# The first four attention pairs of a layer take their rows straight from the projected parts in SBUF

## The chip, the cores and the metric

The kernel runs on one core of a Trainium2 chip. The metric is the device time of one execution in microseconds (us): the median of three runs before the change is 1721.19 us (1714.81 to 1726.53).

## What is computed

The input x is 2 batches of 1024 tokens with 128 features. The reference applies an ffn layer to it, then a top-k attention layer, then the same ffn layer again. The part of the ffn layer that the change touches is its causal attention with 16 heads of 8 features:

```
q, k, v = split(x @ w_qkv)                     # 16 heads x 8 features each
scores  = q . k / sqrt(8), causal mask         # 1024 x 1024 for each of 2 x 16 heads
attn    = softmax(scores);  o = (attn . v) @ w_o
h       = layernorm(x + o);  then 8 experts (w1, gelu, w2), weighted by the top 2 of the gate
```

The kernel runs the ffn layer twice (c = 0 and c = 1), the top-k attention lies between the two.

## The kernel before, in words

**Pairs.** Two heads of one batch are a pair, and a layer has 16 pairs. A pair's queries and keys stand as "rows" of two SBUF tiles, QB and KB, [128 x 1024] each (ring of RING = 4, tiles ffn_65 to 68 and ffn_69 to 72 in the trace's names). A number is split in two fp32r parts (high and low), and the product of all parts is made by 32 contraction rows for each head: for one head QB holds each of 2 x 8 part rows twice, KB holds its 16 part rows in two copies. Behind them are 3 rows in which the row maxima are subtracted.

**How the rows come to be.** L880 and L882 multiply x by w_qkv; ScalarE (L1242) writes the high parts and VectorE (L1561, counter low_done) the low parts to qparts and kparts (ffn_49 and ffn_50), in which feature h*8+d of head h is a partition. After four of its eight blocks the first batch is complete (two of them are the queries, two the keys). `sp_spill` writes the parts of one batch to memory (q_rows, k_rows: 2 MB for a batch), and `sp_rows` loads a pair's rows from there, with the repetition that the layout wants: for each head 128 KB into QB (L475), 128 KB into KB (L476) and three zero rows (L477). A last transfer (L482) copies the pair's 72 KB of values into VS. `sp_rows` of the first pair waits until the whole spill of batch 0 has landed.

**The work on a pair.** Pass 1 (`pe_pass1`, L769 and L776; 9 units) makes scores whose maxima VectorE takes (L1468, L1478). VectorE then reduces them to row maxima (L1486), GpSimd splits these into three bf16 parts (L687 to L694), TensorE turns them (L785), ScalarE copies them (L1216, counter mt_ready), and SyncE's queue stores them to QB's three rows (`sp_maxrows`, L489, two transfers of 12 KB). Only then pass 2 may run: `pe_scores` (L802), exp on ScalarE (L1207), the causal cut on GpSimd (L708) and `pe_values` (L824).

**What sets the order at a layer's start.** TensorE runs the 9 pass 1 units of pair 0 and 4 of pair 1, then turns pair 0's maxima and waits for their rows. From there the pieces of pair n's pass 2 and pair n+1's and n+2's pass 1 alternate in a fixed order. All transfers of this part are issued by SyncE, in program order, to one hardware queue (q1) that is served by 16 DMA engines; a transfer that is issued later stands behind the earlier ones on the engines that it uses. In layer 0 SyncE also issues before all this the experts' first weights, the top-k attention's weights, and bb1: the experts' biases, 4096 elements of 4 bytes each (L564). In layer 1 it issues the first experts' weights (1 MB) ahead of the spill.

**GpSimd's part.** `pool_fill` clears QB and KB of all four ring places and writes ones into KB's three rows, one place after the other (counter filled).

## Time and profile before

| | |
|---|---|
| median of three runs | 1721.19 us |
| profiled execution, its own time | 1717.98 us |
| its span | 1715.8 us |
| TensorE busy | 1417.6 us, 83% of the span |
| VectorE / ScalarE / GpSimd busy | 1242.0 / 998.4 / 447.7 us |
| chain that ended last | PE 60%, DVE 11%, ACT 9%, DMA 6%, issue 6%, SPq 3% |

The span is the profiled execution's time from its first to its last instruction. TensorE is the engine that sets most of the end, but what this change touches are two stretches in which it stands still: in layer 0 between 20 and 85 us, in layer 1 between 1186 and 1249 us. Times in rows are us from the span's start. "PEclk" is the granted share of TensorE's clock (1.00 is 2.4 GHz, 0.50 is 1.2 GHz).

### The profile page before, as it was taken

What the parts mean: (1) busy time and instruction counts of PE and PEld (TensorE: products, weight loads), DVE (VectorE), ACT (ScalarE), POOL (GpSimd) and SP (SyncE); (2) the same over time, 40 slices, a digit from 0 to 9 for tenths busy, and PEclk for the clock granted to TensorE, in tenths of its full rate; (3) what the DMA queues carried; (4) which work ended last, traced back from release to release, by engine and by line L of the source; (5) the groups of instructions that cost most, each with busy time, mean ns of one, the idle gap of its engine ahead of it and who ended that gap; (6) DMA issues with size and microseconds to landing.
All of it is one profiled execution on the core that took longest, in us unless ns stands there. A gap on an engine that the chain in (4) does not pass through costs nothing.

```text
span 1715.8 us, 32136 instructions
## 1 busy us (share of the span) xinstructions
PE 1417.6 (83%) x10708; PEld 921.1 (54%) x10708; DVE 1242.0 (72%) x2568; ACT 998.4 (58%) x1812; POOL 447.7 (26%) x751
## 2 busy tenths in 40 slices
PE   3699998699994764699899999994599999599994
PEld 2355554477773321456565655673355554467773
DVE  3688884677778577777878787753578885667777
ACT  2266667288883672346556545552166667388883
POOL 4122222000001113345555544623122223100000
PEclk8599999699997965899999988997599999789998
DMA  5211110022201245122132212212211110022100
GB/s 145 90 47 45 46 47 3 9 91 74 73 25 42 60 114 124 42 60 63 37 82 64 67 34 58 76 32 86 101 45 45 45 47 8 2 99 74 73 25 25
DMA packets 63686, 99.67 MB, mean 58 GB/s; under 512 B 20011, under 2 KB 43507, under 8 KB 61494
## 3 DMA queue, kind: packets, MB, share of 16 engines
q1 hardware_dynamic: 53910, 80.42, 15.1%
q0 software_dynamic: 8192, 16.79, 3.8%
q8 instruction: 73, 1.20, 0.3%
q10 hardware_dynamic: 1456, 0.80, 0.2%
q14 instruction: 55, 0.45, 0.1%
HBM read 73.39 MB, written 10.69 MB: 49 GB/s over the span
## 4 chain that ended last, share of the span: by engine, by line
PE 60%; DVE 11%; ACT 9%; issue 6%; DMA 6%; DVEq 3%; SPq 3%; ACTq 1%; POOL 1%; POOLq 0%
PE twin L977 10%; PE twin L967 7%; PE twin L824 6%; PE twin L1140 5%; PE twin L802 5%; PE twin L769 4%; ACT arena L1207 4%; DMA ffn<-arena 3%; DVEq L1812 2%; PE twin L1168 2%; PE twin L1156 2%; PE twin L1121 2%; ACT experts L1282 2%; PE twin L1184 2%; PE twin L776 1%
## 5 line engine op out<-in xcount | busy, mean ns | idle before, releaser
L1207 ACT ACTIVATE arena<-twin 128x1024 f32<-128x1024 f32 x288 | 293.8, 1024 | 171.2 <-PE twin L802 169.4
L747 POOL DMA_INDIRECT arena<-kv_rows,IDX x256 | 251.8, 984 | 312.0 <-PE twin L1187 151.9
L1478 DVE TENSOR_REDUCE arena<-twin 128x8 f32<-128x1024 f32 (+1 forms) x160 | 195.3, 1225 | 76.7 <-PE twin L769 42.2
L1527 DVE TENSOR_TENSOR experts<-arena,experts 128x512 fp32r<-128x512 f32 x256 | 171.6, 689 | 71.1 <-ACT experts L1282 71.1
L1280 ACT ACTIVATE arena<-twin,bias 128x512 f32<-128x512 f32 x256 | 185.6, 725 | 46.1 <-PE twin L967 46.0
L967 PE MATMUL twin<-experts,experts 128*128 128x512 f32 x768 | 196.3, 402 | 7.7 <-ACT experts L1282 5.7
L769 PE MATMUL twin<-ffn,ffn 64*128 64x128 f32 (+3 forms) x1152 | 155.2, 352 | 49.9 <-DMA arena<-arena 27.4
L1468 DVE TENSOR_REDUCE arena<-twin 128x2 f32<-128x1024 f32 x128 | 153.0, 1222 | 51.2 <-PE twin L769 47.7
L1282 ACT ACTIVATE experts<-twin,bias 128x512 fp32r<-128x512 f32 x256 | 186.9, 730 | 0.0
L977 PE MATMUL twin<-experts,experts 128*128 128x512 f32 x768 | 182.3, 389 | 0.0
L708 POOL TENSOR_SCALAR_AFFINE_SELECT arena<-arena 128x256 f32<-128x256 f32 x256 | 99.6, 407 | 306.8 <-ACT arena L1207 306.8
L967 PEld LDWEIGHTS twin<-experts,experts 128*128 128x128 f32 x768 | 143.2, 192 | 55.4 <-ACT experts L1282 22.8
L802 PE MATMUL twin<-ffn,ffn 64*128 64x128 f32 (+3 forms) x960 | 148.4, 373 | 26.2 <-DMA ffn<-arena 21.8
L642 POOL TENSOR_TENSOR rstd<-vareps,neghalf 128x8 f32<-128x8 f32 x14 | 23.4, 1675 | 541.7 <-DVE vareps L1457 541.7
L824 PE MATMUL twin<-arena 128*32 128x128 f32 (+3 forms) x1920 | 158.7, 431 | 2.8 <-POOL arena L708 1.8
L977 PEld LDWEIGHTS twin<-experts,experts 128*128 128x128 f32 x768 | 144.1, 188 | 30.5
L769 PEld LDWEIGHTS twin<-ffn,ffn 64*128 64x128 f32 x1152 | 97.0, 202 | 83.5 <-ACT arena L1207 36.4
L802 PEld LDWEIGHTS twin<-ffn,ffn 64*128 64x128 f32 x960 | 79.1, 188 | 107.0 <-issue 62.8
L1876 DVE TENSOR_TENSOR HN<-twin,RT 96x512 f32<-96x512 f32 x128 | 87.0, 680 | 59.2 <-PE twin L1140 51.2
L1429 ACT ACTIVATE ATT<-twin,col 128x256 f32<-128x256 f32 x128 | 60.6, 473 | 106.6 <-DVE col L1885 105.5
L1435 ACT ACTIVATE ATT<-ATT,inverse 128x256 f32<-128x256 f32 x128 | 64.6, 505 | 80.5 <-DVE inverse L1890 79.9
L1140 PE MATMUL twin<-XN,arena 128*128 128x512 bf16 x408 | 104.0, 395 | 0.2 <-DVE HN L1876 0.2
(259 smaller groups left out, 2225.0 us busy)
## 6 DMA issues: line engine op xcount, KB each, us to landing
arena<-wt_rows SPq DMA_DIRECT2D x16, 1024.0 KB, 4.8
arena<-in_L_ffn_w SPq DMA_DIRECT2D x32, 256.0 KB, 5.2
ffn<-q_rows SPq DMA_DIRECT2D x64, 128.0 KB
ffn<-k_rows SPq DMA_DIRECT2D x64, 128.0 KB
XT<-idx_rows SPq DMA_DIRECT2D x16, 512.0 KB, 3.9
q_rows<-ffn SPq DMA_DIRECT2D x8, 512.0 KB, 4.9
...
```

The costliest lines, as they stand in the source:

```text
L747: pool.indirect_dma_start(G[d % GR][:, g, :], None, kv_rows, bass.IndirectOffsetOnAxis(ap=IDX[:, q, k * GB + g:k * GB + g + 1], axis=0))\
L769: m = pe.matmul(bank[2 * slot + s][:, at * P:(at + blocks) * P], QB[buf][r, q * P:(q + 1) * P], KB[buf][r, k0 * P:(k0 + blocks) * P], star ...
L802: x = pe.matmul(bank[2 * slot + s][:, at * P:(at + 4 - p) * P], KB[buf][r, kc * P:(kc + 1) * P], QB[buf][r, (4 * g + p) * P:(4 * g + 4) * ...
L824: m = pe.matmul(bank[6][r:r + STRIP, p * P:], VS[buf][:, v:v + STRIP], PT[(UNITS * buf + u) % PT_RING][:, s, at * P:(at + 4 - p) * P], sta ...
L967: m = pe.matmul(bank[f][:, :], W1R[buf][w][:, f * P:(f + 1) * P], XR[x][:, tb * BANK:(tb + 1) * BANK], start=((w, x) == pairs[0]), stop=(( ...
L977: m = pe.matmul(bank[4 + k][:, :], W2R[buf][w][:, f, :], H1R[k][x][:, f, :], start=(f == 0 and (w, x) == pairs[0]), stop=(f == FC - 1 and ...
L1140: m = pe.matmul(o[:, :], TAB[part][:, 4 * b + c, :], OH[OH_AT[x][c] % OHR][:, :], start=(c == 0 and part == 0), stop=(c == n - 1 and part ...
L1207: act.activation(PT[(UNITS * buf + u) % PT_RING].rearrange("p s n -> p (s n)"), twin[2 * u % S_RING][:, :], ACT.Exp, scale=float(HD) ** -0 ...
L1280: act.activation(H1[tb % 2][:, f, :], bank[f][:, :], ACT.Gelu_apprx_tanh, bias=bias1[buf][:, f:f + 1])
L1282: act.activation(H1R[tb % 2][0][:, f, :], bank[f][:, :], ACT.Gelu_apprx_tanh, bias=bias1[buf][:, f:f + 1]).then_inc(gelu_done, 1)
L1478: dve.tensor_reduce(to, scores.rearrange("p (s t k) -> p s t k", s=2, t=to.shape[2]), AX_X, ALU.max).then_inc(max_done, 1)
L1527: dve.tensor_tensor(H1R[tb % 2][1][:, f, :], H1[tb % 2][:, f, :], H1R[tb % 2][0][:, f, :].bitcast(F32), ALU.subtract)\
```

## The change

For pairs 0 to 3 of a layer the rows no longer come from memory. `sp_parts` copies them from qparts and kparts in SBUF to QB and KB: 8 partitions of a head are the source of each transfer, 16 rows of 4 KB its destination, so a pair takes 8 transfers of 64 KB (and no zero rows, since the fill has cleared them). `sp_first` waits only for the fill of its ring place and for the queries' and then the keys' low parts. The copies of pairs 0, 1 and 2 and their values go ahead of the spill of batch 0; bb1 (layer 0) goes behind that spill and ahead of pair 0's maxima; pair 3 and the spill of batch 1 go behind pair 0's maxima; in layer 1 the first experts' weights go behind these. Then SyncE waits for both spills before it enters its loop, whose first transfers are pair 1's maxima. New counters (`first_loaded`) let TensorE start pass 1 of pairs 0 and 1 without their values, for which it waits ahead of the first `pe_values`. In layer 1 ring place 0 is cleared by ScalarE (`act_fill`) as soon as x_ready allows, and GpSimd, which no longer does this, has a drain ahead of its layer.

The diff:

```diff
--- before.py
+++ after.py
@@ -177,6 +177,15 @@
 CUT = [u for u in range(UNITS) if diagonals(u)]
 VSIZE = (2 * TB - 1) * VW + STRIP
 ROW_LOADS = 16 * (2 * 3 + 1)
+FIRST_LOADS = 16 * 2 * 2 * PARTS
+VISITS = PAIRS // RING
+
+
+def rows_target(c, buf, visit):
+
+
+    first = 16 if buf < 2 else 16 + FIRST_LOADS
+    return (ROW_LOADS * (VISITS - 1) + first) * c + first + ROW_LOADS * visit
 
 ARENA = 36992 * 4
 
@@ -409,7 +418,7 @@
 
 
         x_loaded, const_loaded, w_loaded, bb1_loaded, sel_w_loaded = (sem(n) for n in ("x_loaded", "const_loaded", "w_loaded", "bb1_loaded", "sel_w_loaded"))
-        setup_done, filled, masks_ready = sem("setup_done"), sem("filled"), sem("masks_ready")
+        setup_done, filled, first_filled, masks_ready = sem("setup_done"), sem("filled"), sem("first_filled"), sem("masks_ready")
 
         var_ready, rstd_ready = sem("var_ready"), sem("rstd_ready")
         xn_ready, h_ready = sem("xn_ready"), sem("h_ready")
@@ -419,6 +428,7 @@
         zeroed, zero_stored, cut_done = (sem(n) for n in ("zeroed", "zero_stored", "cut_done"))
         v_done, va_ready = sem("v_done"), sem("va_ready")
         rows_spilled = [sem(f"rows_spilled{b}") for b in range(B)]
+        first_loaded = [sem(f"first_loaded{i}") for i in range(2)]
         rows_loaded = [sem(f"rows_loaded{i}") for i in range(RING)]
 
         s1_done, max_done, top_ready, mb_ready, mt_done, mt_ready, maxrow_loaded = (sem(n) for n in ("s1_done", "max_done", "top_ready", "mb_ready", "mt_done", "mt_ready", "maxrow_loaded"))
@@ -462,12 +472,37 @@
         w1_d, w2_d = ffn["w1"], ffn["w2"].rearrange("e (c p) d -> e p c d", p=P)
 
 
+        def sp_parts(sp, it, s, which, done):
+
+            h, n = slice((2 * it + s) * HD, (2 * it + s + 1) * HD), HD * PARTS
+            for i in range(PARTS):
+                r = TILE * s + i * n
+                if which == 0:
+                    to, rows = QB[it], qparts[h, i, 0:L].unsqueeze(1).broadcast_to([HD, PARTS, L])
+                else:
+                    to, rows = KB[it], kparts[h, :, 0:L]
+                sp.dma_start(to[r:r + n, :].bitcast(F32), rows.bitcast(F32)).then_inc(done, 16)
+
+        def sp_values(sp, it, buf):
+            va = VA[:, :, :, :, :].rearrange("p a s k d -> p (a s k d)")
+            n = 2 * TB * VW
+            sp.dma_start(VS[buf][:, 0:n], va[:, bass.ds(it * n, n)]).then_inc(rows_loaded[buf], 16)
+
+        def sp_first(sp, c, it, done):
+
+            if c and it == 0:
+                sp.wait_ge(first_filled, 1)
+            else:
+                sp.wait_ge(filled, RING * c + it + 1)
+            for which in range(2):
+                sp.wait_ge(low_done, 8 * c + 2 * (which + 1))
+                for s in range(2):
+                    sp_parts(sp, it, s, which, done)
+
         def sp_rows(sp, c, it, buf):
 
-            g = PAIRS * c
-            if not isinstance(it, int) or c:
-                sp.wait_ge(pv_done, PV0 + len(GROUPS) * (g + it - RING + 1))
-            pair = slice(it, it + 1) if isinstance(it, int) else bass.ds(it, 1)
+            sp.wait_ge(pv_done, PV0 + len(GROUPS) * (PAIRS * c + it - RING + 1))
+            pair = bass.ds(it, 1)
             for s in range(2):
                 r = TILE * s
                 q = q_rows[pair, s].rearrange("a r d t -> (a r d) t").unsqueeze(1).broadcast_to([PARTS * HD, PARTS, L])
@@ -475,11 +510,7 @@
                 sp.dma_start(QB[buf][r:r + PRODS, :].bitcast(F32), q).then_inc(rows_loaded[buf], 16)
                 sp.dma_start(KB[buf][r:r + PRODS, :].bitcast(F32), k).then_inc(rows_loaded[buf], 16)
                 sp.dma_start(QB[buf][r + PRODS:r + ROWS, :].bitcast(F32), zero_rows).then_inc(rows_loaded[buf], 16)
-            if isinstance(it, int):
-                sp.wait_ge(va_ready, NG * (c + 1))
-            va = VA[:, :, :, :, :].rearrange("p a s k d -> p (a s k d)")
-            n = 2 * TB * VW
-            sp.dma_start(VS[buf][:, 0:n], va[:, bass.ds(it * n, n)]).then_inc(rows_loaded[buf], 16)
+            sp_values(sp, it, buf)
 
         def sp_maxrows(sp, c, it, buf):
 
@@ -513,25 +544,29 @@
             sp.dma_start(WB[buf], row.rearrange("a t -> (a t)").partition_broadcast(P)).then_inc(wb_loaded[buf], 16)
 
         def sp_ffn(sp, c):
-            if c:
-
-                sp.wait_ge(x_ready, 2)
-                sp_expert(sp, c, 0, 0)
-                sp_expert(sp, c, 1, 1)
-
             if c == 0:
                 sp.wait_ge(zeroed, 1)
                 sp.dma_start(zero_rows, PT[0][0:MAXROWS, :, :].rearrange("p s n -> p (s n)")).then_inc(zero_stored, 16)
+            for it in range(2):
+                sp_first(sp, c, it, first_loaded[it])
+            sp.wait_ge(va_ready, NG * (c + 1))
+            for it in range(2):
+                sp_values(sp, it, it)
+            sp.wait_ge(zero_stored, 16)
+            sp_first(sp, c, 2, rows_loaded[2])
+            sp_values(sp, 2, 2)
             sp_spill(sp, c, 0)
-            sp.wait_ge(zero_stored, 16)
-            sp.wait_ge(rows_spilled[0], (PARTS + 1) * 16 * (c + 1))
-            for k in range(RING):
-                if k == 2:
-                    sp_spill(sp, c, 1)
-                sp.wait_ge(filled, RING * c + k + 1)
-                sp_rows(sp, c, k, k)
-            sp.wait_ge(rows_spilled[1], (PARTS + 1) * 16 * (c + 1))
+            if c == 0:
+                sp_biases(sp)
             sp_maxrows(sp, c, 0, 0)
+            sp_first(sp, c, 3, rows_loaded[3])
+            sp_values(sp, 3, 3)
+            sp_spill(sp, c, 1)
+            if c:
+                for e in range(2):
+                    sp_expert(sp, c, e, e)
+            for b in range(B):
+                sp.wait_ge(rows_spilled[b], (PARTS + 1) * 16 * (c + 1))
             with sp.Fori(1, PAIRS // RING) as i:
                 for k in range(RING):
                     sp_maxrows(sp, c, i * RING + k - (RING - 1), (k + 1) % RING)
@@ -561,6 +596,8 @@
                 sp.dma_start(dst, src).then_inc(sel_w_loaded, 16)
             for x in range(P // HALF):
                 sp.dma_start(delta_col[x * HALF:(x + 1) * HALF, 0:1], attn["raw_delta"].rearrange("(i a) -> i a", a=1)).then_inc(delta_loaded, 16)
+
+        def sp_biases(sp):
             sp.dma_start(bb1[:, :, :], ffn["bb1"].rearrange("e (f p) -> p e f", p=P), allow_slow_non_contiguous=True).then_inc(bb1_loaded, 16)
 
 
@@ -644,7 +681,7 @@
         def pool_ffn(pool, c):
             ln = (0, 4)[c]
             if c:
-
+                pool.drain()
                 pool.wait_ge(x_ready, 2)
             pool_rstd(pool, ln)
             pool_fill(pool, c)
@@ -666,12 +703,15 @@
             pool.memset(MB.bitcast(F32), 0.0)
             for buf in range(RING):
                 pool.memset(VS[buf][:, 2 * TB * VW:], 0.0)
-                pool.memset(QB[buf][:, :].bitcast(F32), 0.0)
-                pool.memset(KB[buf][:, :].bitcast(F32), 0.0)
-                pool.drain()
-                for s in range(2):
-                    pool.memset(KB[buf][TILE * s + PRODS:TILE * s + ROWS, :].bitcast(F32), 1.0)
-                pool.drain()
+                if c == 0 or buf:
+                    pool.memset(QB[buf][:, :].bitcast(F32), 0.0)
+                    pool.memset(KB[buf][:, :].bitcast(F32), 0.0)
+                    pool.drain()
+                    for s in range(2):
+                        pool.memset(KB[buf][TILE * s + PRODS:TILE * s + ROWS, :].bitcast(F32), 1.0)
+                    pool.drain()
+                else:
+                    pool.drain()
                 pool.memset(spare[:, 3:4], float(c)).then_inc(filled, 1)
 
         def pool_maxrows(pool, c, it):
@@ -760,7 +800,10 @@
 
             n = PAIRS * c + it
             if u == 0:
-                pe.wait_ge(rows_loaded[buf], ROW_LOADS * (PAIRS // RING * c + visit + 1))
+                if isinstance(it, int) and it < 2:
+                    pe.wait_ge(first_loaded[it], FIRST_LOADS * (c + 1))
+                else:
+                    pe.wait_ge(rows_loaded[buf], rows_target(c, buf, visit))
             at = 0
             for j, (qt, k0, blocks) in enumerate(PASS1[u]):
                 for s in range(2):
@@ -896,6 +939,8 @@
             for u in range(HALFWAY):
                 pe_scores(pe, c, 0, 0, u, PAIRS)
                 pe_next(pe, c, 1, 1, u, u + EARLY, 0)
+            for it in range(2):
+                pe.wait_ge(rows_loaded[it], rows_target(c, it, 0))
             pe_values(pe, c, 0, 0, 0)
             run_steps(pe, pe_step, c)
 
@@ -1232,8 +1277,21 @@
                 for u in range(2, HALFWAY):
                     act_exp(act, c, it + 1, one, u)
 
+        def act_fill(act):
+
+            act.wait_ge(x_ready, 2)
+            for rows in (QB[0], KB[0]):
+                act.activation(rows[:, :], spare[:, 0:1].broadcast_to([P, L]), ACT.Copy)
+            act.drain()
+            for s in range(2):
+                r = slice(TILE * s + PRODS, TILE * s + ROWS)
+                m = act.activation(KB[0][r, :], neghalf[r, 0:1].broadcast_to([ROWS - PRODS, L]), ACT.Copy, scale=-2.0)
+            m.then_inc(first_filled, 1)
+
         def act_ffn(act, c):
             n_turn = (0, 4)[c]
+            if c:
+                act_fill(act)
             act_turn(act, n_turn)
             for n in range(8):
                 act.wait_ge(qk_done, 8 * c + n + 1)
```

SyncE's queue in layer 0, before, from the last small loads to the values of pair 0 (ffn_49 and ffn_50 are the parts, ffn_65 and ffn_69 QB and KB of pair 0):

```order
L563 DMA delta_col<-in_L_attn_raw_delta 16x1 x8
L564 DMA bb<-in_L_ffn_bb 128x32x1
L524 DMA zero_rows<-arena 3x1024 [waits zeroed]
L496 DMA q_rows<-ffn_49 16x8x1024 [waits low_done]
L496 DMA q_rows<-ffn_49 16x8x1024
L497 DMA k_rows<-ffn_50 256x1x1024
L475 DMA ffn_65<-q_rows 32x1x1024 [waits filled,rows_spilled0,zero_stored]
L476 DMA ffn_69<-k_rows 32x1x1024
L477 DMA ffn_65<-zero_rows 3x1024
```

The same place in the changed kernel, with what stands ahead of pair 0's maxima (L520, which was L489):

```order
L549 DMA zero_rows<-arena 3x1024
L484 DMA ffn_65<-ffn_49 16x1x1024 x4
L484 DMA ffn_69<-ffn_50 16x1x1024 x4
L484 DMA ffn_66<-ffn_49 16x1x1024 x4
L484 DMA ffn_70<-ffn_50 16x1x1024 x4
L489 DMA arena<-arena 128x144 x2
L484 DMA ffn_67<-ffn_49 16x1x1024 x4
L484 DMA ffn_71<-ffn_50 16x1x1024 x4
L489 DMA arena<-arena 128x144
L527 DMA q_rows<-ffn_49 16x8x1024 x2
L528 DMA k_rows<-ffn_50 256x1x1024
L601 DMA bb<-in_L_ffn_bb 128x32x1
```

The copies of three pairs now lead, and the spill of batch 0 and the biases have moved behind them.

SyncE's queue in layer 1 of the changed kernel (in layer 0 the expert rows are missing there), behind pair 0's maxima up to pair 1's (ffn_68 and ffn_72 are QB and KB of pair 3, ffn_66 QB of pair 1; at the branch the queue waits for both spills):

```order
L484 DMA ffn_68<-ffn_49 16x1x1024 x4
L484 DMA ffn_72<-ffn_50 16x1x1024 x4
L489 DMA arena<-arena 128x144
L527 DMA q_rows<-ffn_49 16x8x1024 x2
L528 DMA k_rows<-ffn_50 256x1x1024
L536 DMA arena<-in_L_ffn_w 128x512
L537 DMA arena<-in_L_ffn_w 128x4x128
L536 DMA arena<-in_L_ffn_w 128x512
L537 DMA arena<-in_L_ffn_w 128x4x128
L570 UNCONDITIONAL_BRANCH
L570 ISA
L520 DMA ffn_66<-arena 3x8x128 x2
```

Before, only the loop's branch stood between pair 0's maxima and pair 1's; now 8 copies, a spill, expert weights and the wait for both spills do.

## Rows read from the trace of the kernel before

**Rows 1.** Chain of waits, layer 0: start us, us, what
```profile
26.68 7.16 DMA k_rows<-ffn
37.68 6.54 DMA arena<-arena
44.36 0.81 PE twin L769 x2
45.27 4.62 DVE arena L1468 x4
59.98 8.66 DMA ffn<-arena
68.69 0.81 PE twin L802 x2
```
**Rows 2.** Chain of waits, layer 1
```profile
1206.95 0.81 PE twin L769 x2
1222.22 9.36 DMA ffn<-arena
1248.49 0.50 PE twin L802 x2
1260.00 0.85 SPq L489
1260.89 2.18 DMA ffn<-arena
```
**Rows 3.** Timeline, layer 0: start us, us, engine, line, op
```profile
21.94 0.69 DVE L1561 TENSOR_TENSOR ffn<-twin,ffn 128x512 fp32r<-128x512 f32 x1 [0.18 <-ACT ffn L1242]
22.27 0.42 SPq L564 DMA_DIRECT2D bb<-in_L_ffn_bb  x1
22.58 0.10 POOL L675 MEMSET spare<- 128x1 f32 x1
26.26 3.73 PE L886 MATMUL twin<-w_qkv,XT 128*128 128x128 f32 x32
27.35 3.48 ACT L1248 ACTIVATE arena<-twin 128x128 f32<-128x128 f32 x16 [0.29 <-PE twin L886]
59.07 1.67 SPq L489 DMA_DIRECT2D ffn<-arena  x2
...
81.98 1.49 SPq L489 DMA_DIRECT2D ffn<-arena  x2
85.05 0.50 PE L802 MATMUL twin<-ffn,ffn 64*128 64x512 f32 x2
```
**Rows 4.** Timeline, layer 1
```profile
1185.88 0.69 DVE L1561 TENSOR_TENSOR ffn<-twin,ffn 128x512 fp32r<-128x512 f32 x1 [0.17 <-ACT ffn L1242]
1189.67 1.93 POOL L673 MEMSET ffn<- 3x1024 f32 x2 [5.37 <-issue]
1191.29 3.48 ACT L1248 ACTIVATE arena<-twin 128x128 f32<-128x128 f32 x16 [0.29 <-PE twin L886]
```
**Rows 5.** Costliest groups of the page: ScalarE's copies of 1024 columns
```profile
L1207 ACT ACTIVATE arena<-twin 128x1024 f32<-128x1024 f32 x288 | 293.8, 1024 | 171.2 <-PE twin L802 169.4
```
**Rows 6.** DMA queue q1, 338.0 to 342.0 us (store of wt_rows): packets, MB, share
```profile
q1 hardware_dynamic: 16, 0.07, 13.8%
```
**Rows 7.** DMA, 596.8 to 604.4 us (copies of 32 partitions): tenths in 40 slices; q1
```profile
DMA  0000009693994997959499394987949949897992
q1 hardware_dynamic: 474, 1.32, 78.4%
```
**Rows 8.** Windows: us; busy by engine; PEclk, DMA share, GB/s
```profile
34.00:44.00 10.00, 0.00 (x0) 0.00 (x0) 0.00 (x0) 0.00 (x0) 0.86 (x2) 0.50 0.33 102
61.00:67.00 6.00, 0.00 (x0) 0.00 (x0) 0.00 (x0) 0.00 (x0) 0.00 (x0) 0.50 0.13 53
28.00:33.00 5.00, 2.00 (x18) 1.80 (x17) 0.00 (x0) 2.54 (x13) 4.61 (x8) 1.00 0.94 362
23.00:26.00 3.00, 3.00 (x12) 2.08 (x12) 2.49 (x4) 2.19 (x4) 2.85 (x4) 1.00 0.78 10
```

## The prediction

> **What bounds the kernel now.** I read first the chain of waits for the two layer starts, then the timeline there, then the DMA queue in stretches where few partitions or few engines work, since the change trades one kind of transfer for another.
>
> The chain shows in either layer the same two holes in TensorE's work. The first is the trip through memory: the spill lands 7.2 us after its last issue, and after SyncE has issued the rows another 6.5 us pass, so pass 1 starts at 44.36 in layer 0 and at 1206.95 in layer 1 [rows 1, 2]. The projections' last results for it, the values, are copied by 30.83 and 1194.77 (27.35 + 3.48, 1191.29 + 3.48) [rows 3, 4]. So 13.5 and 12.2 us are waited for rows. The second hole is pair 0's maxima: issued at 59.07, they land after 8.66 us, and pass 2 starts at 68.69; in layer 1 the wait is 9.36 us and ends at 1231.6 [rows 1 to 3]. In the steady loop the same store is done 3.0 us after the start of its issue (0.85 + 2.18) [rows 2]. The rest, about 6 us, is queueing: from 61 to 67 the DMA engines are 0.13 busy at 53 GB/s, that is 2.1 of 16 engines at 25 GB/s each [rows 8]. The maxima land when this tail ends. A few engines with a backlog hold up a small transfer; this is the thing to watch in the new order.
>
> Pair 1's maxima are issued at 81.98, and TensorE needs them at 85.05, which is 16.4 us after 68.69; in layer 1 this is 16.9 us, at 1248.49 [rows 1 to 3].
>
> **What one pair costs in the new way.** A pair is 8 transfers of 64 KB, 512 KB in all, each from 8 partitions. SyncE needs 0.42 us for one plain issue and 0.75 for one of the maxima's (1.49 for two) [rows 3]; I take 0.5, so issue alone is 4 us for a pair. The transfer itself is the larger: the trace has a store from 8 partitions, wt_rows, 8 rows of 8 KB. It holds 13.8% of 16 engines for 4 us, 8.8 engine-us, so each of 8 engines needs 1.1 us for 8 KB, or 7.4 GB/s an engine [rows 6]. The copies with 32 partitions on both sides move 1.32 MB in 0.784 x 16 x 7.6 = 95 engine-us, 13.9 GB/s an engine, though 16 work [rows 7]; the tail above has 25. So few partitions slow each engine. Per 64 KB 1.1 us gives 8.8 us a pair. Scaling the 32-partition copies by partitions (1.32 MB in the 6.5 us in which bytes flow is 203 GB/s, a quarter is 51) gives 10.3 us. **I take T = 9.3 us a pair**, nearer to the store, which is the same shape; ends 8.8 and 10.3. A much lower T, about 5 us, holds if only the destination's partitions count (16 rows, half of 203 GB/s), since no row shows a read from 8 partitions with an SBUF target.
>
> The Trainium skill, SBUF — State Buffer, section "Door 1: The DMA port swizzle", says that bandwidth goes by how many of 16 ports the partitions reach, 27.2 GB/s each; 8 neighbouring partitions reach two. By that an estimate for a pair is 9.6 us and the gain below would be 2.4 us smaller. The rows above agree with its direction (7.4, 13.9 and 25 GB/s an engine). It speaks against this change: the copies avoid memory, but not two ports.
>
> **Layer 0.** The queue is free at 22.3, as the bias load (issue at 22.27) is gone from there; the queries are complete at 22.63 and ring place 0 is filled at 22.68 [rows 3]. First copy issued at 22.8, first bytes 1.2 us later, as in the copies' stretch, which begins at an issue and shows no bytes for 1.1 us [rows 7]: 24.0. Pair 0 is through at 33.3, landed 0.6 us later, pass 1 starts at **33.9 instead of 44.36**. Pair 1 is there at 43.2, needed nine units after the start, at VectorE's 1.15 us a unit [rows 1] 10.4 us, at 44.3: just in time. Pass 1 runs at VectorE's pace as before. TensorE stops at 30.0 (26.26 + 3.73) [rows 3], so its clock will have fallen again when pass 1 starts, as it is 0.50 in 34 to 44 [rows 8]; I take nothing from that.
>
> Pair 0's maxima are ready 14.7 us after the start of pass 1 (59.07 against 44.36), at 48.6. They stand behind three pairs (27.9 us from 24.0: 51.9), three value copies (0.2 us each at 362 GB/s [rows 8]: 52.5), the spill (2.1 MB over 16 engines, 131 KB on each, at 25 GB/s 5.3 us: 57.8) and the biases, which keep all engines at 0.78 for 3 us at 10 GB/s and a little beyond, 2.8 us in all [rows 8]: 60.6. Plus 0.9 to land: **61.5 instead of 68.69, 7.2 us earlier**. Most of the 10.5 us won at pass 1 is kept, none is added, since the copies now are the backlog.
>
> Then comes the new wait. Behind pair 0's maxima (60.9) stand pair 3 (70.2), its values and the second spill (75.7), and SyncE waits for both spills before it may issue pair 1's maxima: free at 76.3, landed 3.0 us later, 79.3. By the old distance they are needed at 61.5 + 16.4 = 77.9. So TensorE gets there at 79.3 instead of 85.05: **5.7 us gained in layer 0**. Queued behind that wait are the rows of pair 4, which ring place 0 needs much later. From there the loop goes on as before.
>
> **Layer 1.** The queries are complete at 1186.57 (1185.88 + 0.69) [rows 4]; bytes from 1187.8. Pair 0 at 1197.7: pass 1 starts 9.2 us earlier. Three pairs 1215.7, values and spill 1221.6, landed 1222.5 against 1231.6: 9.1 us. Then pair 3, values, spill 1236.7, expert weights (1 MB, 64 KB an engine, 2.6 us) 1239.3, or by the other way SyncE free at 1237.3 and 3.0 us more: pair 1's maxima land at 1240.3 against 1248.49: **8.2 us gained**. The drain of 5.37 us that GpSimd has within its fill (the idle time ahead of L673 [rows 4]) moves to where it waits for x_ready; with or without it ring place 1 is filled by about 1192, pair 1's turn on the engines comes at 1197. ScalarE's fill of place 0, two instructions of 1024 columns (1.02 us each by L1207 [rows 5]) and two small ones, lies ahead of the transposes, where ScalarE waits for XN, and costs nothing; if that cover were gone, it would be 2 to 3 us once. The moved expert weights are needed only behind the attention, 200 us later: nothing. The dropped zero rows and smaller waits: nothing.
>
> **Sum.** 1717.98 (the profiled execution's own time) - 5.7 - 8.2 = 1704.1. Each us of T is worth 8 us here: four pairs in either layer stand ahead of pair 1's maxima. T = 8.8 gives 1700, T = 10.3 gives 1712. The profiled execution is 3.2 us under the median of the runs; I predict **1706 us**, own range 1698 to 1714.
>
> **Rivals.**
>
> *The source's partitions don't count (T about 5).* Then pass 1 starts when the values are copied, at 30.9 and 1194.9. Pair 0's maxima are ready at 45.6 and land at 49.2 in layer 0 (24.0 + 15 + 9.6, rounded up by issue), in layer 1 at 1212.6 (1209.6 + 3.0), and pair 1's find both spills landed. Gain 19.5 + 19 = 38.5 us: **1680 us**. For it: the store in rows 6 goes to memory, where the first packets of a transfer could be slow for their own reason. Against it: the two series above fit a source limit. 0.2.
>
> *The copies eat the gain (T about 11).* If each of the 8 transfers loses 0.2 us as the engines change to the next, T = 11 and the sum is 1704 + 8 x 1.7 = 1718, **no change, 1721 as a median**. For it: a pair's two reads of one partition follow each other, and 16 target rows are few as well. Against: the copies of rows 7 follow each other as closely and keep the engines over 0.9 busy at their rate. 0.13.
>
> *Slower: the copies fall on too few engines.* The tail of [rows 8] shows that a transfer can run on 2 engines; if a copy ran on one at 25 GB/s, T = 21: layer 0's pair 0 maxima land at 24.0 + 63 + 9.6 = 96.6, pair 1's at 126, 41 us late, layer 1 39 us late: **about 1798 us**. It decides from T = 13.3 on, where the loss passes 1%. Against: wt_rows, with 8 rows, ran on 8. 0.07.
>
> The Trainium skill, DMA: Bandwidth & Descriptors, section "Why a DMA increments its semaphore by 16 and not by 1", has the number of engines as the largest up to 16 that divides both sides' slowest dimensions; that is 8 here and would rule the last rival out. No run here shows it for these copies.
>
> **Chances.** The forecast has 0.6. A measurement of this kernel tells about 1% (17 us, bounds 1704.0 and 1738.4) from no change. The forecast lies 2 us above the lower bound: of its 0.6 I put 0.2 under it. So faster is 0.2 + 0.2 = 0.4; within 1% are the forecast's other 0.4, the second rival's 0.13 and 0.01 of the last, 0.54; slower 0.06. The range takes in the forecast's bounds, most of the first rival and the second: 1678 to 1720.
>
> **What would show it.** In the changed profile: pass 1 (L769's successor) starts near 34 and 1198, not 31 and 1195; DMA share about 0.5 at some 55 GB/s from 24 to 52, as eight engines work on the copies; pair 0's maxima waited for from about 49 to 61.5; SyncE waiting for q_rows or k_rows near 76 and 1237 ahead of pair 1's maxima; the steady loop unchanged. The prediction fails if those GB/s are over 90 (first rival) or under 45, or if TensorE waits in places that these steps don't name.

## The result, and the profile after

| | before | after |
|---|---|---|
| median | 1718.07 us (4 runs, 1714.81 to 1726.53) | 1697.66 us (4 runs, 1694.58 to 1703.17) |
| profiled execution, its own time | 1717.98 us | 1697.26 us |
| its span, mean granted clock | 1715.8 us, 0.900 | 1695.2 us, 0.904 |
| ratio of the medians | | 0.9885, 95% interval 0.9861 to 0.9909 |

The time falls by 1.15%, 20.4 us by the medians and 20.7 by the profiled executions, against 13.9 in the sum of the forecast. It lies inside the predicted range (1678 to 1720), 8 us under the predicted value and 0.3 us under the forecast's own narrower range (1698 to 1714). The lines of the kernel have moved: pass 1 is L812 (was L769), pass 2 L845 (L802), the turn of the maxima L828 (L785), the new copies L484, the value copies L489 (L482), the maxima's issue L520 (L489), the spill L527 and L528, the bias load L601, the expert loads L536 and L537.

Layer 0 in the timeline, SyncE's row of issues (start us, us, engine, line, operation, out<-in, count) with TensorE's first matmul of each pass, each of which shows in brackets how long TensorE stood still and for what:

```profile
22.90 13.41 SPq L484 DMA_DIRECT2D ffn<-ffn  x16
...
37.80 6.59 SPq L484 DMA_DIRECT2D ffn<-ffn  x8
44.43 0.59 SPq L489 DMA_DIRECT2D arena<-arena  x1
45.06 1.46 SPq L527 DMA_DIRECT2D q_rows<-ffn  x2
46.56 1.64 SPq L528 DMA_DIRECT2D k_rows<-ffn  x1
48.24 2.04 SPq L601 DMA_DIRECT2D bb<-in_L_ffn_bb  x1
50.33 5.64 SPq L520 DMA_DIRECT2D ffn<-arena  x2
56.08 6.29 SPq L484 DMA_DIRECT2D ffn<-ffn  x8
```
```profile
32.53 0.96 PE L812 MATMUL twin<-ffn,ffn 64*128 64x512 f32 x6 [2.36 <-DMA ffn<-ffn]
...
57.43 0.79 PE L845 MATMUL twin<-ffn,ffn 64*128 64x512 f32 x2 [11.18 <-DMA ffn<-arena]
...
75.82 0.50 PE L845 MATMUL twin<-ffn,ffn 64*128 64x512 f32 x2 [1.34 <-DMA ffn<-arena]
```

They answer to [rows 1, 3]. The first hole, 13.5 us ahead of pass 1, is down to 2.4 us. The second, pair 0's maxima, is still there: 11.18 us. It is SyncE that now has almost no gap. A pair's 8 copies are 6.3 to 6.9 us of issue (0.84 us each in the first 16), three pairs fill it from 22.9 to 44.4, then come the value copy, the spill and the bias load. The two issues of the maxima take 5.64 us, where two of them took 1.67 before [rows 3]. The pause is the bias load's transfer (windows of the change; busy us of PE, PEld, DVE, ACT, POOL; granted clock, DMA share, GB/s):

```profile
54.00:54.50 0.50, 0.00 (x0) 0.00 (x0) 0.00 (x0) 0.00 (x0) 0.00 (x0) 0.50 1.23 9
54.50:55.00 0.50, 0.00 (x0) 0.00 (x0) 0.00 (x0) 0.00 (x0) 0.00 (x0) 0.50 0.55 4
55.00:55.50 0.50, 0.00 (x0) 0.00 (x0) 0.00 (x0) 0.00 (x0) 0.00 (x0) 0.50 0.10 1
```

The spill's bytes are through at about 54, then the DMA engines work at 4 to 9 GB/s, which is the bias load with its 4-byte elements. The first of the maxima's issues ends at 55.11, when this transfer is all but over.

Behind that the chain of waits shows what the second spill does to pair 1's maxima (start us, us, what):

```profile
64.94 6.97 DMA k_rows<-ffn
71.95 0.44 issue
72.59 0.86 SPq L520
73.51 2.19 DMA ffn<-arena
75.82 0.50 PE twin L845 x2
```

Layer 1 has the same picture without the bias load (timeline, SyncE; then TensorE; then ScalarE's fill of ring place 0):

```profile
1179.74 13.17 SPq L484 DMA_DIRECT2D ffn<-ffn  x16
...
1205.19 2.98 SPq L520 DMA_DIRECT2D ffn<-arena  x2
...
1225.96 1.73 SPq L520 DMA_DIRECT2D ffn<-arena  x2
```
```profile
1189.38 0.96 PE L812 MATMUL twin<-ffn,ffn 64*128 64x512 f32 x6 [2.34 <-DMA ffn<-ffn]
...
1211.25 0.79 PE L845 MATMUL twin<-ffn,ffn 64*128 64x512 f32 x2 [7.85 <-DMA ffn<-arena]
...
1229.24 0.50 PE L845 MATMUL twin<-ffn,ffn 64*128 64x512 f32 x2 [1.00 <-DMA ffn<-arena]
```
```profile
1165.31 2.00 ACT L1284 ACTIVATE ffn<-spare 128x1024 fp32r<-128x1024 f32 x2 [20.14 <-DVE X L1797]
```

The windows answer to [rows 8] (us; busy us of PE, PEld, DVE, ACT, POOL; granted clock, DMA share, GB/s). While only copies run, the DMA engines are under half busy; the spill runs at 330 GB/s with all of them:

```profile
24.00:36.00 12.00, 8.38 (x53) 6.20 (x51) 6.23 (x9) 5.59 (x20) 10.16 (x16) 0.90 0.46 74
```
```profile
47.00:53.00 6.00, 0.00 (x0) 0.00 (x0) 1.87 (x2) 0.00 (x0) 0.00 (x0) 0.51 1.00 330
```

**How the kernels are compared below.** The stretch between the layers (the selection and the attention over it) differs by some us from run to run and by much more from chip to chip: e1 to e4 ran on one chip, on which the kernel before takes 1838.61 us, e5 to e8 on a second (1840.02), e9 to e12 on a third (1716.96; one execution there took 3167.67 us and is left out of the ratios). The ratios are taken on one chip each. The kernel before has a profile only from the first measurement. So I count in each layer from the start of ScalarE's copy of the values (27.35 and 1191.29 before [rows 3, 4], 27.53 and 1184.40 after) to pass 1, to pass 2, and to pair 1's pass 2. The last of these is what a layer gains at its start. How well a place repeats is shown by kernels that start alike: e6, which is the change but for one fill, has on the second chip the places of the change within 0.5 us, and e4 to e6 and e10 differ from the change by up to 0.9 us where their edit touches nothing.

| kernel | layer 0: pass 1, pass 2, pair 1 | layer 1 | ratio to before (95%) |
|---|---|---|---|
| before | 17.01, 41.34, 57.70 | 15.66, 40.33, 57.20 | |
| the change | 5.00, 29.90, 48.29 | 4.98, 26.85, 44.84 | 0.9885 (0.9861 to 0.9909) |
| e10 the change again | 5.06, 30.02, 48.77 | 5.03, 27.24, 45.74 | 0.9896 (0.9870 to 0.9921) |
| e1 heads alternate | 3.74, 26.63, 44.36 | 3.71, 23.51, 40.92 | 0.9826 (0.9782 to 0.9869) |
| e2 moves alone | 15.96, 40.55, 57.90 | 15.66, 41.47, 58.63 | 0.9995 (0.9972 to 1.0018) |
| e3 copies alone | 6.15, 28.44, 45.97 | 5.05, 27.16, 44.20 | 0.9863 (0.9834 to 0.9892) |
| e4 bias last | 5.08, 27.32, 44.59 | 4.96, 27.52, 45.38 | 0.9900 (0.9866 to 0.9934) |
| e5 wait for one spill | 5.03, 30.31, 47.78 | 4.99, 26.94, 44.86 | 0.9896 (0.9857 to 0.9935) |
| e6 fill by GpSimd | 5.11, 30.13, 48.53 | 4.96, 27.30, 45.24 | 0.9920 (0.9895 to 0.9945) |
| e7 two issuers | 5.06, 25.47, 43.55 | 5.13, 22.39, 42.26 | 0.9907 (0.9870 to 0.9945) |
| e8 spill behind maxima | 5.11, 22.60, 46.28 | 4.96, 22.39, 47.07 | 0.9934 (0.9910 to 0.9959) |
| e9 half the bytes | 3.58, 26.73, 44.11 | 3.57, 23.93, 41.21 | one run |
| e11 all, pair 3 first | 3.73, 25.86, 43.27 | 3.75, 25.49, 43.10 | 0.9830 (0.9804 to 0.9856) |
| e12 all, pair 3 behind | 3.76, 21.06, 39.02 | 3.65, 21.22, 39.44 | 0.9826 (0.9795 to 0.9858) |

By these places the change gains 9.4 us in layer 0 and 12.4 in layer 1, 21.8 together, of which the profiled execution shows 20.7.

Whether a gain lasts to the end of a layer's attention is read from the last row of pass 2 in each layer, counted from the same start (timeline, layer 1: before, then e12):

```profile
1459.22 0.50 PE L802 MATMUL twin<-ffn,ffn 64*128 64x256 f32 x4
```
```profile
1430.27 0.50 PE L845 MATMUL twin<-ffn,ffn 64*128 64x256 f32 x4
```

| kernel | last row of pass 2: layer 0, layer 1 | gain there | gain at pair 1 | by the ratio (95%) |
|---|---|---|---|---|
| before | 268.98, 267.93 | | | |
| the change | 260.97, 255.54 | 20.4 | 21.8 | 20 (16 to 24) |
| e1 | 255.53, 251.53 | 29.9 | 29.6 | 32 (24 to 40) |
| e7 | 254.83, 255.07 | 27.0 | 29.1 | 17 (10 to 24) |
| e8 | 264.60, 259.03 | 13.3 | 21.6 | 12 (8 to 17) |
| e11 | 255.01, 255.52 | 26.4 | 28.5 | 29 (25 to 34) |
| e12 | 250.68, 253.29 | 32.9 | 36.4 | 30 (24 to 35) |

For the change, e1 and e11 the gain at pair 1 lasts to within 2.1 us; e12 loses 3.5 us of it behind pair 1 and e8 8.3. e7 keeps all but 2.1 us in the attention, but its whole time shows 10 us less than that, for which no run here has the reason.

### The profile page after: what moved, and what is told of

Same layout as the page of the kernel before. It is cut to its first block, busy times and chain, and to the rows that moved or that the text cites. A ratio compares the mean times of both kernels' runs of the same rounds, so it can differ in the third digit from the quotient of the medians.

```text
span 1695.2 us, 32157 instructions
## 1 busy us (share of the span) xinstructions
PE 1417.5 (84%) x10708; PEld 920.9 (54%) x10708; DVE 1242.1 (73%) x2568; ACT 1003.4 (59%) x1816; POOL 444.2 (26%) x747
## 4 chain that ended last, share of the span: by engine, by line
PE 59%; DVE 11%; ACT 9%; SPq 6%; issue 6%; DMA 4%; DVEq 3%; ACTq 1%; POOL 1%; POOLq 0%
PE twin L1022 10%; PE twin L1012 7%; PE twin L867 5%; PE twin L1185 5%; PE twin L845 4%; PE twin L812 4%; ACT arena L1252 4%; SPq L484 3%; DVEq L1870 2%; DMA ffn<-arena 2%; PE twin L1213 2%; PE twin L1201 2%; ACT experts L1340 2%; PE twin L1166 2%; PE twin L1229 2%
## 5 line engine op out<-in xcount | busy, mean ns | idle before, releaser
L1252 ACT ACTIVATE arena<-twin 128x1024 f32<-128x1024 f32 x288 | 294.1, 1024 | 173.7 <-PE twin L845 171.7
L812 PE MATMUL twin<-ffn,ffn 64*128 64x128 f32 (+3 forms) x1152 | 154.3, 350 | 27.6 <-ACT arena L1252 13.8
L845 PE MATMUL twin<-ffn,ffn 64*128 64x128 f32 (+3 forms) x960 | 148.7, 374 | 27.0 <-DMA ffn<-arena 22.3
L845 PEld LDWEIGHTS twin<-ffn,ffn 64*128 64x128 f32 x960 | 79.3, 189 | 109.2 <-issue 63.9
L1934 DVE TENSOR_TENSOR HN<-twin,RT 96x512 f32<-96x512 f32 x128 | 87.0, 680 | 61.5 <-PE twin L1185 53.6
L812 PEld LDWEIGHTS twin<-ffn,ffn 64*128 64x128 f32 x1152 | 96.1, 200 | 60.8 <-ACT arena L1252 36.1
```

Of the source, the lines that this page charges most:

```text
L812: m = pe.matmul(bank[2 * slot + s][:, at * P:(at + blocks) * P], QB[buf][r, q * P:(q + 1) * P], KB[buf][r, k0 * P:(k0 + blocks) * P], star ...
L845: x = pe.matmul(bank[2 * slot + s][:, at * P:(at + 4 - p) * P], KB[buf][r, kc * P:(kc + 1) * P], QB[buf][r, (4 * g + p) * P:(4 * g + 4) * ...
L1252: act.activation(PT[(UNITS * buf + u) % PT_RING].rearrange("p s n -> p (s n)"), twin[2 * u % S_RING][:, :], ACT.Exp, scale=float(HD) ** -0 ...
```

## The experiments

**What sets the pace of the copies (e1, e9, e7).** In the change each head's two copies, which read the same 8 partitions, stand side by side. e1 alternates the heads:

```diff
-        def sp_parts(sp, it, s, which, done):
+        def sp_parts(sp, it, i, which, done):
...
-            for i in range(PARTS):
+            n = HD * PARTS
+            for s in range(2):
+                h = slice((2 * it + s) * HD, (2 * it + s + 1) * HD)
...
-                for s in range(2):
-                    sp_parts(sp, it, s, which, done)
+                for i in range(PARTS):
+                    sp_parts(sp, it, i, which, done)
```

> The two copies that read the same 8 partitions are no longer neighbours in the queue: each is followed by the other head's. In the changed kernel 16 copies take 13.41 us, 0.84 each, in layer 0 and 13.17 in layer 1, and pass 1 starts at 32.53 and 1189.38. Theory A (the copies go at the pace at which SyncE issues them, 0.72 us median): nothing moves, 16 copies in 13.4 us +-0.4, pass 1 at 32.5, the whole time within 2 us. Theory B (the source's partitions still hold the copies up, and the issue is held back by the queue): neighbours that read different partitions overlap, 16 copies in about 10 us, three pairs 5 us earlier, pass 2 of pair 0 at 52 instead of 57.4, time about 1687 us.

Measured: in between. 16 copies took 11.74 us instead of 13.41, and by the places pass 2 came 3.3 us earlier in both layers, pair 1's 3.9. The chain of waits of the change (first fence) and of e1 (second) shows it copy by copy, one row for each issue:

```profile
29.71 0.67 SPq L484
...
30.43 0.84 SPq L484
...
31.31 0.67 SPq L484
...
32.02 0.73 SPq L484
```
```profile
29.99 0.67 SPq L485
...
30.70 0.67 SPq L485
...
31.42 0.67 SPq L485
```

In the change some issues take longer, up to 1.13 us, in e1 each of these takes 0.67, one every 0.72 us. So there is a floor, and the change's order puts 0.1 us a copy on it. In e1 two things alternate at once: the 8 partitions that are read, and the half of QB or KB that is written. That the shared source is the cause is likely, since the change's neighbours write different rows already, but no run alternates one without the other. e9 halves the bytes and leaves the number and the order of the copies:

```diff
-                    to, rows = QB[it], qparts[h, i, 0:L].unsqueeze(1).broadcast_to([HD, PARTS, L])
+                    to, rows = QB[it], qparts[h, i, 0:L // 2].unsqueeze(1).broadcast_to([HD, PARTS, L // 2])
...
-                    to, rows = KB[it], kparts[h, :, 0:L]
-                sp.dma_start(to[r:r + n, :].bitcast(F32), rows.bitcast(F32)).then_inc(done, 16)
+                    to, rows = KB[it], kparts[h, :, 0:L // 2]
+                sp.dma_start(to[r:r + n, 0:L // 2].bitcast(F32), rows.bitcast(F32)).then_inc(done, 16)
```

> The changed kernel with as many copies, but each moves only the first 512 of 1024 columns (the rest of the first four pairs' operands stays zero, so their attention is not the reference's). Theory A (SyncE's issue sets the pace): 8 copies still take 5.8 us or more, 16 copies 11.7 or more, pass 1 starts within 1 us of its old place. Theory B (the source's partitions and engines do, per byte): 8 copies fall to about 3.5 us, 16 to about 7, or to the issue's own 0.4 us each.

Measured (timeline of e9, SyncE, and below it e1):

```profile
22.97 11.74 SPq L484 DMA_DIRECT2D ffn<-ffn  x16
```
```profile
23.93 11.74 SPq L485 DMA_DIRECT2D ffn<-ffn  x16
```

The same 11.74 us with 32 KB a copy as with 64: the floor does not go by bytes, and theory A holds for the pace. Its "within 1 us" for pass 1 did not hold (3.58 against 5.00), and pass 1 no longer waits for the copies there, but for ScalarE's copy of the values, which ends 3.48 us after its start:

```profile
31.00 0.97 PE L812 MATMUL twin<-ffn,ffn 64*128 64x512 f32 x6 [0.94 <-ACT arena L1306]
```

So pass 1 can't come before about 3.6 in the table, and e1, e11 and e12 are near that. The number of copies is the same in e9, so a fixed cost of a copy on the DMA engines is left as a rival to SyncE's issue. e7 tests that one, with a second engine that issues pair 2's copies while SyncE is still at pair 1's:

```diff
-            sp_first(sp, c, 2, rows_loaded[2])
...
                 m.then_inc(va_ready, 1)
+            sp_first(act, c, 2, rows_loaded[2])
             act_maxrow(act, c, 0)
```

> The changed kernel with the 8 copies of pair 2 issued by ScalarE behind its copy of the values, where it is idle for 15 us, beside SyncE's of pair 1. Theory A (SyncE's issue, 0.8 us a copy, sets the pace of the copies): SyncE reaches the spill 6.6 us earlier, pair 0's maxima are issued when they are ready, pass 2 at +23.5 instead of +29.90 in layer 0 and +22.5 instead of +26.85 in layer 1, pair 1's at +41 and +40: about 12 us off the time. Theory B (the partitions and the engines set it): two queues take turns, the copies end as late as before, the gain is under 3 us.

Measured (timeline of e7, SyncE and ScalarE's queue):

```profile
22.59 14.49 SPq L484 DMA_DIRECT2D ffn<-ffn  x16
```
```profile
30.75 7.50 ACTq L484 DMA_DIRECT2D ffn<-ffn  x8
```

24 copies are out by 38.25 instead of 44.39, and each engine loses about a tenth of its pace to the other. While both issue, the DMA engines move more than they did for SyncE alone (window of e7, read as the windows above; the change had 74 GB/s from 24 to 36):

```profile
31.00:37.00 6.00, 3.36 (x16) 1.84 (x16) 4.11 (x4) 0.00 (x0) 3.55 (x5) 0.66 0.46 107
```

So a copy's cost on the DMA engines was not the floor; one queue's issue was. By the places pass 2 comes 4.4 and 4.5 us earlier, pair 1's 4.7 and 2.6. Theory A named the cause, but its size was too large by 5 us: in layer 0 the maxima's two issues still took 4.91 us behind the bias load, in layer 1 SyncE waited 8.2 us for the second spill ahead of pair 1's. The ratio of the whole times, 0.9907, is not below the change's 0.9885, so for the kernel's time e7 shows no gain over the change.

**What the moves are worth (e2, e3).** e2 makes only the moves in the kernel before, e3 only the copies:

```diff
-            if c:
-                sp.wait_ge(x_ready, 2)
-                sp_expert(sp, c, 0, 0)
-                sp_expert(sp, c, 1, 1)
...
+            if c == 0:
+                sp_biases(sp)
+            if c:
+                for e in range(2):
+                    sp_expert(sp, c, e, e)
             with sp.Fori(1, PAIRS // RING) as i:
...
+        def sp_biases(sp):
```

> The kernel before, rows still through memory, with the bias load and layer 1's first expert loads put behind pair 0's maxima. Theory A (the gain is the copies'): the queue is free 0.45 us earlier for the issue and the zero rows' issue, 2.58 us behind the bias load, becomes short, so the spill and all behind it come 2.3 us earlier in layer 0 (pass 1 at 42.0 instead of 44.36, pair 1's pass 2 at 82.7 instead of 85.05), nothing in layer 1: 1715.7 against 1718.0. Rival (the moves carry much of it, since the expert weights share the engines with the spill): layer 1's pass 1 comes 2 us or more earlier too, time under 1712.

```diff
         def sp_ffn(sp, c):
+            if c:
+                sp.wait_ge(x_ready, 2)
+                sp_expert(sp, c, 0, 0)
+                sp_expert(sp, c, 1, 1)
...
-            if c == 0:
-                sp_biases(sp)
             sp_maxrows(sp, c, 0, 0)
...
-            if c:
-                for e in range(2):
-                    sp_expert(sp, c, e, e)
...
-        def sp_biases(sp):
```

> The changed kernel with the bias load and layer 1's expert loads back in their old places. Theory A (the bias load costs a block of 2 to 5 us on SyncE wherever it stands): the first copy is issued near 25.4 instead of 22.9, pass 1 at 35.0 instead of 32.5, but pair 0's maxima are no longer stuck at their issue: pass 2 at 56 to 57.5 (57.43 in the changed kernel), pair 1's pass 2 at 74 to 75 (75.82); layer 1 unchanged within 1 us; time 1696 to 1699. Rival (the move of the bias load is worth its 2.8 us on the path): pass 2 at 59.5 or later, time 1700 or more.

Measured: the moves alone bring pass 1 of layer 0 only 1.1 us forward and pair 1's pass 2 not at all (57.90 against 57.70); the ratio is 0.9995. Layer 1 is 1.1 and 1.4 us later at pass 2 and pair 1. The 2.3 us expected at pass 1 were not there, because the spill waits for the parts of batch 0, which the kernel before has complete at 24.34 (timeline, the fourth low part) while its spill is issued at 25.36; no more than 1.0 us could be won:

```profile
23.65 0.69 DVE L1561 TENSOR_TENSOR ffn<-twin,ffn 128x512 fp32r<-128x512 f32 x1 [0.17 <-ACT ffn L1242]
```

The copies alone bring all of it and, by the places, more: with the bias load back ahead of the copies pass 1 is 1.2 us later, but pair 1's pass 2 in layer 0 is 2.3 us earlier than in the change. So the move of the bias load costs time at these places (e3's ratio, 0.9863, can't be told from the change's). Expert loads ahead or behind: 44.20 against 44.84, with 44.84 to 45.74 in the four profiles (the change, e5, e6, e10) that start alike, decides nothing about them.

**What holds pair 0's maxima (e4, e8).** e4 puts the bias load behind the loop over the pairs:

```diff
             sp_spill(sp, c, 0)
-            if c == 0:
-                sp_biases(sp)
             sp_maxrows(sp, c, 0, 0)
...
+            if c == 0:
+                sp_biases(sp)
             for it in range(PAIRS - RING + 1, PAIRS):
```

> The changed kernel with the bias load behind the loop over the pairs. In the changed kernel the issue of pair 0's maxima took 4.78 us right behind the bias load (50.33), and pass 2 started at 57.43. Theory A (that issue was held by the bias load): maxima issued at 48.3 to 49.8, landed at the end of the spill's bytes, pass 2 at 54.0, pair 1's at 70.4 instead of 75.82: 5.4 us off the time, about 1692. Rival (the spill's backlog held the maxima, the issue only waited in its place): pass 2 at 57 or 56, the time less than 2 us lower.

Measured, in the chain of waits: the change (first fence; L601 is the bias load, L520 the maxima's issue) and e4:

```profile
48.24 2.04 SPq L601
...
50.33 4.78 SPq L520
...
55.17 0.81 SPq L520
```
```profile
49.48 1.76 SPq L520
...
51.29 4.23 DMA ffn<-arena
...
55.56 0.81 PE twin L845 x2
```

Without the bias load in front, the issue of the two maxima falls from 5.64 to 3.08 us in all, but they then land 4.2 us after it, in the spill's tail, where 2.2 is usual. Pass 2 comes 2.6 us earlier and pair 1's 3.7, two thirds of the 5.4 expected. Both causes are there: the issue held behind the bias load, and the spill's backlog. Layer 1, which the edit doesn't touch, came 0.7 and 0.5 us later in this profile, and the ratio of the whole times, 0.9900, shows no gain over the change. e8 takes spill and bias load from in front of the maxima, and waits for the first spill alone:

```diff
-            sp_spill(sp, c, 0)
-            if c == 0:
-                sp_biases(sp)
             sp_maxrows(sp, c, 0, 0)
             sp_first(sp, c, 3, rows_loaded[3])
             sp_values(sp, 3, 3)
+            sp_spill(sp, c, 0)
+            if c == 0:
+                sp_biases(sp)
             sp_spill(sp, c, 1)
...
-            for b in range(B):
-                sp.wait_ge(rows_spilled[b], (PARTS + 1) * 16 * (c + 1))
+            sp.wait_ge(rows_spilled[0], (PARTS + 1) * 16 * (c + 1))
...
+                sp.wait_ge(rows_spilled[1], (PARTS + 1) * 16 * (c + 1))
```

> The changed kernel with the first spill and the bias load behind pair 0's maxima, pair 3 and its values, and with the wait for the first spill alone ahead of pair 1's maxima. Theory A (the backlog of the spill and the bias load is what holds pair 0's maxima): they are issued when ready, pass 2 at +22 to +23 instead of +29.90 in layer 0 and +22 to +23 instead of +26.85 in layer 1; pair 1's maxima then stand behind both spills and, in layer 1, behind the issue of the expert loads: +42 and +42.5 instead of +48.29 and +44.84, 8 to 9 us off the time. Rival (the maxima lie behind the copies of pair 2 themselves): pass 2 not before +26 in layer 0.

Measured: pass 2 at 22.60 and 22.39, as theory A has it; no three pairs' copies hold the maxima, 7.3 and 4.5 us were the spill's and the bias load's. But pair 1's pass 2 came at 46.28 and 47.07, not 42 and 42.5: 2.0 us earlier than in the change in layer 0 and 2.2 later in layer 1. The chain of waits of layer 0:

```profile
60.02 1.95 SPq L601
...
62.01 4.61 SPq L527
...
69.46 0.96 SPq L520
...
70.48 4.14 DMA ffn<-arena
```

The 4.6 us behind the bias load hit the second spill's first issue now (0.6 to 1.2 without), and in layer 1 the expert loads were still being issued when the maxima were ready. A stall in SyncE's queue moves to whoever is next.

**The wait for both spills (e5).**

```diff
-            for b in range(B):
-                sp.wait_ge(rows_spilled[b], (PARTS + 1) * 16 * (c + 1))
+            sp.wait_ge(rows_spilled[0], (PARTS + 1) * 16 * (c + 1))
...
                     sp_rows(sp, c, i * RING + k, k)
+                sp.wait_ge(rows_spilled[1], (PARTS + 1) * 16 * (c + 1))
```

> The changed kernel, but ahead of pair 1's maxima SyncE waits for the first spill alone; the second is waited for only ahead of pair 8's rows. Counted from ScalarE's copy of the values, pair 1's pass 2 stands at +48.29 in layer 0 of the changed kernel and at +44.84 in layer 1, its maxima are ready at about +43.2 and +40.4. Theory A (the wait holds them): issued 1.5 us earlier, pair 1's pass 2 at +46.6 and +43.8, 2.5 us in all. Rival (they would stand behind the second spill's bytes on the same engines, so the wait costs nothing): +48 and +44.8, no gain.

Measured: 47.78 and 44.86, that is 0.5 and 0.0 us. The rival holds: the wait is in the chain, but almost nothing stands behind it.

**ScalarE's fill (e6).**

```diff
-            if c and it == 0:
-                sp.wait_ge(first_filled, 1)
-            else:
-                sp.wait_ge(filled, RING * c + it + 1)
+            sp.wait_ge(filled, RING * c + it + 1)
...
-                if c == 0 or buf:
+                if True:
...
-            if c:
-                act_fill(act)
```

> The changed kernel with ring place 0 filled by GpSimd in layer 1 as in layer 0, and ScalarE's fill gone; GpSimd's drain stays moved. Theory A (ScalarE's fill is worth nothing, since GpSimd's four places take 4.1 us each from 1175.3, place 0 is done at 1179.4 and the first copy is issued at 1179.74 anyway): layer 1's pass 1 stays within 0.5 us of +4.98 after the copy of the values, the time within 2 us of the changed kernel's. Rival (the later places come 4.1 us later and pair 1's or 2's copies wait for them): pass 2 in layer 1 later than +26.85 by 2 us or more.

Measured: pass 1 in layer 1 at 4.96 against 4.98, pass 2 at 27.30 against 27.24 in e10 (26.85 in the first profile of the change). ScalarE's fill brings nothing and costs nothing.

**The gains together (e10, e11, e12).** e11 is the change with this order on SyncE, the heads alternated as in e1 and pair 2 issued by ScalarE as in e7; e12 has the line of pair 3 behind that of the maxima:

```diff
-            sp_first(sp, c, 2, rows_loaded[2])
-            sp_values(sp, 2, 2)
             sp_spill(sp, c, 0)
-            if c == 0:
-                sp_biases(sp)
-            sp_maxrows(sp, c, 0, 0)
             sp_first(sp, c, 3, rows_loaded[3])
+            sp_maxrows(sp, c, 0, 0)
+            sp_values(sp, 2, 2)
             sp_values(sp, 3, 3)
             sp_spill(sp, c, 1)
-            if c:
-                for e in range(2):
-                    sp_expert(sp, c, e, e)
...
+            if c == 0:
+                sp_biases(sp)
+            else:
+                for e in range(2):
+                    sp_expert(sp, c, e, e)
             for it in range(PAIRS - RING + 1, PAIRS):
```

> The changed kernel itself, beside the two combinations on the same chip. Its ratio to the kernel before was 0.9885 when first measured; on this chip 0.988 to 0.992 is expected, and its places as then: pass 2 at +29.9 and +26.9, pair 1's at +48.3 and +44.8 from the copy of the values.

> The gains put together: heads alternate, ScalarE issues pair 2, bias and expert loads behind the loop, pair 3's copies between the first spill and pair 0's maxima, the second spill behind the maxima. Theory A (each of these waits is issue or backlog): maxima issued when ready, pass 2 at +22.5 in both layers instead of +29.9 and +26.9; the second spill has landed when pair 1's maxima are ready, so pair 1's pass 2 at +39 instead of +48.29 and +44.84: 15 us less than the changed kernel, ratio about 0.980 to 0.981 to the kernel before. Rival (pair 3's copies hold the maxima instead, as one more backlog): pass 2 at +25 or later, pair 1's at +42: 9 us less.

> The same with pair 3's copies behind pair 0's maxima. Theory A: pass 2 at +22.4, but the second spill lands only at about +37, and SyncE waits for it: pair 1's pass 2 at +40.5 to +41, 1.5 us in each layer behind the other combination. Rival (pair 3's copies do hold the maxima in the other one): this one is ahead by 1 us or more.

Measured on one chip: the change repeats (e10: 0.9896 and the places within 0.9 us, as expected). The change 1700.86 us (1696.26 to 1705.32), e11 1689.89 (1685.02 to 1693.56), e12 1690.04 (1684.95 to 1690.91). Both are 0.6% faster than the change, and their runs don't overlap with its. By the places e11 got its rival's numbers, and e12, expected 1.5 us a layer behind e11, is ahead of it, as its rival says: pair 3's copies behind the spill were issued in 8.9 us instead of 5.9 and held the maxima (timeline of e11, where L485 are the copies, L521 the maxima's issue and L490 a value copy; below it e12, with the maxima first):

```profile
41.41 8.88 SPq L485 DMA_DIRECT2D ffn<-ffn  x8
50.33 1.66 SPq L521 DMA_DIRECT2D ffn<-arena  x2
```
```profile
46.97 1.74 SPq L521 DMA_DIRECT2D ffn<-arena  x2
48.75 0.60 SPq L490 DMA_DIRECT2D arena<-arena  x1
49.46 5.89 SPq L485 DMA_DIRECT2D ffn<-ffn  x8
```

e12 has the best starts, 9.3 and 5.4 us ahead of the change's first profile, and TensorE's wait for pair 0's maxima in layer 0 is down to 3.58 us. That e11, 4.3 and 3.7 us behind it at the starts, has the same median, I can't explain from the starts. By the last row of pass 2 the lead is 4.3 and 2.2 us, and in their profiles the stretch from pair 1's pass 2 of layer 0 to layer 1's copy of the values took 1103.6 us in e11 and 1108.8 in e12, and 1106.2 to 1108.6 in before, the change and e10. Such a difference between runs is as large as what is compared.

## Why the prediction held, and where it was off

*The chance.* Faster than 0.99 had 0.4, within 1% 0.54. The ratios 0.9885 and 0.9896 lie just under that border, on the side that had the smaller chance; the direction was right and the size 8 us short. By its own sum the forecast's median is 1704.1 + 3.2 = 1707.3; the 1706 that it gives is 1.3 lower without a reason.

*T, the price of a pair, was the step that was off.* It was taken as 9.3 us, from transfer; measured are 6.6 to 6.7 us, from issue. It was the issue that set the pace, which the forecast had at 4 us a pair and under the transfer. Of the terms, the store of 8 rows to memory [rows 6] did not carry over: the copies ran at 74 GB/s with the engines 0.46 busy from 24 to 36, which is 10 GB/s an engine, not 7.4. And the issue was not 0.5 us a copy but 0.73 at least (e9), with 0.1 on top in the change's order (e1). T is 5.86 to 5.87 us with half the bytes and with the heads alternated alike, so with the heads alternated no transfer limit shows at 64 KB a copy. The first rival's "about 5" was nearer in T, but its 38.5 us of gain did not come. The sign that the prediction set for itself, over 90 or under 45 GB/s, saw neither: 74 against some 55 foreseen.

The Trainium skill, SBUF — State Buffer, section "Door 1: The DMA port swizzle", was used for two ports a pair, an estimate of 9.6 us. Its rule counts a transfer's partitions, and one copy reads 8, so two ports; the pair's two heads together lie in 16 partitions, which are four ports and an estimate of 4.8 us. The measured 6.7 us of the change and 5.86 of e1 lie between the two. So the 9.6 does not hold for copies that follow each other, and whether the ports have a part in the 0.1 us a copy, no run here shows.

*Layer 0, pass 1*: 33.9 forecast, 32.53 measured. T alone, 2.6 us less, would have given 31.3; but the last copy of the pair, issued by 29.6, lands and lets TensorE start 2.9 us later, where the sum had 1.2 to the first bytes and 0.6 to land. Two errors partly cancel here. The forecast's clock was off too, without effect: it was granted in full when pass 1 began (1.00 from 32 to 33) and fell to 0.50 at 34. *Pair 0's maxima*: that three pairs, spill and bias load stand ahead of a small transfer is as told; but the three pairs are a backlog of SyncE's issue, not of the DMA engines. Forecast 61.5, measured 57.43, though 3 x 2.7 us less copying makes it 53.4. Of the 4.0 us 3.3 are the spill's: its bytes run at full rate from about 47 to 53, where the sum with the shorter copies ends them at 49.7. They wait for its issue (45.06 to 48.20), which was not counted while the transfers were thought to be the bound. The other 0.7 is the bias load's: the sum gave 3.7 us, 2.8 of transfer and 0.9 to land; measured are 2.1 from 53 to 55.11, when its transfer is all but over, and then 2.3 more, since only then the second of the maxima's transfers was issued. *Pair 1's maxima*: forecast 79.3, measured 75.82. The new wait of SyncE for both spills was there, 6.97 us long, but ended at 72 instead of 76.3, when the maxima were all but ready (they were issued at 72.59); e5 shows that it costs 0.5 us at most.

*Layer 1*: pair 1's pass 2 gained 12.4 us, forecast 8.2, with the same reason. *Costed at nothing*: ScalarE's fill (2.00 us behind 20.14 of idle time), right by e6, and the zero rows, which no run tests alone. The expert loads too: each issue took up to 1.55 us, but in SyncE's wait for the spill; in e8, where the first of them was issued only at 1342.75, they ran to 1348.54 and pair 1's maxima stood behind them. The bias load's move was given 0.4 us of gain at the first copy and 2.8 of cost in the queue; e3 shows 2.3 us lost net at pair 1's pass 2, the same in size, though by way of an issue that stands still.

*The sum.* 13.9 forecast, 21.8 measured at the places, and "each us of T is worth 8" would have given 35 for T = 6.6: once the copies are short, the maxima's own readiness and SyncE's other issues take over. *The rivals*: the slow engines (T = 21) and T = 11 are out by every run. That the gain is the moves' and not the copies', which the prediction did not name, is out by e2.
